# Two attention layers' output stage: turns handed on sooner, x moved in tiles, and every output tile behind the last attention step

## The reference

```python
def _L0_attn_ref(x, w_q, w_k, w_v, w_o):
    ...
    q, k, v = (proj(w_q), proj(w_k), proj(w_v))
    scores = jnp.einsum('bhqd,bhkd->bhqk', q, k) / jnp.sqrt(jnp.float32(D_K))
    attn = jax.nn.softmax(scores, axis=-1)
    out = jnp.einsum('bhqk,bhkd->bhqd', attn, v)
    out = out.transpose(0, 2, 1, 3).reshape(B, S, HIDDEN)
    return jnp.einsum('bse,oe->bso', out, w_o)
...
x = L0_attn_x
x = x + _layernorm(_L0_attn_ref(_layernorm(x, axis=-1), ...), axis=-1)
x = x + _layernorm(_L0_ffn_ref(_layernorm(x, axis=-1), ...), axis=-1)
x = x + _layernorm(_L1_attn_ref(_layernorm(x, axis=-1), ...), axis=-1)
x = x + _layernorm(_L1_ffn_ref(_layernorm(x, axis=-1), ...), axis=-1)
```

## Time and profile before

| | |
|---|---|
| median of 3 runs | 2146.65 us (2146.11 to 2153.83) |
| the profiled execution | 2145.93 us, of which 2144.0 us are the span from its first to its last instruction |
| PE busy | 1921.5 us (90% of the span), 11664 products |
| DVE / ACT / POOL busy | 1422.2 us (66%) / 1142.0 us (53%) / 211.3 us (10%) |
| mean granted clock of PE | 0.958 of full speed |
| DMA | 178.16 MB, mean 83 GB/s |

### The profile page before, as it was taken

One profiled execution on the slowest core, in us unless ns is written; L12 is line 12 of the kernel. 1 busy time (PEld: TensorE's weight loads), 2 busy tenths in 40 slices (PEclk: granted clock), 3 DMA queues, 4 the chain that ended last, 5 costly groups with the idle time before them and its releaser, 6 DMA issues. The chain is left out here.

```text
span 2144.0 us, 31834 instructions
## 1 busy us (share of the span) xinstructions
PE 1921.5 (90%) x11664; PEld 1087.6 (51%) x11664; DVE 1422.2 (66%) x2444; ACT 1142.0 (53%) x2391; POOL 211.3 (10%) x251
## 2 busy tenths in 40 slices
PE   5999999999999999659999999499999999996585
PEld 4864333333333333347888887364444444443463
DVE  5346979999999997354433231567777787763577
ACT  3214777888887887313322221125677777763143
POOL 0000010000000000330010010100100000002313
PEclk9999999999999999879999999699999999998798
DMA  6582443354335431243010100462633444412411
GB/s 202 158 190 74 66 105 69 56 84 76 63 65 82 75 57 39 76 165 100 16 40 1 40 20 0 143 162 68 137 77 79 81 87 90 80 54 76 171 41 59
DMA packets 133434, 178.16 MB, mean 83 GB/s; under 512 B 48244, under 2 KB 59380, under 8 KB 133136
## 3 DMA queue, kind: packets, MB, share of 16 engines
q1 hardware_dynamic: 132896, 175.38, 35.4%
q0 software_dynamic: 384, 0.77, 0.1%
HBM read 111.21 MB, written 64.36 MB: 82 GB/s over the span
## 5 line engine op out<-in xcount | busy, mean ns | idle before, releaser
L927 DVE TENSOR_REDUCE maxesB<-banksB 128x1 f32<-128x1024 f32 x512 | 602.2, 1216 | 92.4 <-PE banksB L993 92.3
L883 ACT ACTIVATE probsB<-banksB 128x512 f32<-128x512 f32 x1024 | 529.6, 602 | 134.8 <-PE banksB L1004 134.7
L924 DVE CUSTOM_DVE_ANT_0 junkG<-banksG,rampG 128x896 bf16<-128x896 f32 (+7 forms) x512 | 368.2, 756 | 104.1 <-PE banksG L993 95.5
L1004 PE MATMUL banksB<-q_stackB,k_stackB 50*128 50x512 f32 x1024 | 405.1, 473 | 7.8 <-DMA q_stackB<-mpartsB 4.8
L883 ACT ACTIVATE probsG<-banksG 128x512 f32<-128x512 f32 (+3 forms) x768 | 326.2, 492 | 119.6 <-PE banksG L1015 68.4
L993 PE MATMUL banksB<-k_stackB,q_stackB 48*128 48x512 f32 x1024 | 345.7, 443 | 3.7
L1004 PEld LDWEIGHTS banksB<-q_stackB,k_stackB 50*128 50x128 f32 x1024 | 167.6, 185 | 270.5 <-ACT probsB L883 228.1
L1004 PE MATMUL banksG<-q_stackG,k_stackG 54*128 54x512 f32 (+3 forms) x768 | 259.6, 413 | 22.0 <-ACT probsG L883 16.5
L1037 PE MATMUL banksB<-probsB,v_onesB 128*32 128x512 f32 x2048 | 276.0, 611 | 0.0
L993 PE MATMUL banksG<-k_stackG,q_stackG 52*128 52x512 f32 (+3 forms) x768 | 248.2, 409 | 11.0 <-DVE maxesG L924 8.2
L993 PEld LDWEIGHTS banksB<-k_stackB,q_stackB 48*128 48x128 f32 x1024 | 155.0, 186 | 85.0 <-DVE maxesB L927 73.8
(11 more groups left out here) (229 smaller groups left out, 2759.5 us busy)
## 6 DMA issues: line engine op xcount, KB each, us to landing
q_stackB<-q_parts SPq DMA_DIRECT2D x96, 128.0 KB, 6.8
k_stackB<-k_parts SPq DMA_DIRECT2D x96, 128.0 KB, 7.2
q_stackG<-q_parts SPq DMA_DIRECT2D x96, 128.0 KB
q_parts<-partsA SPq DMA_DIRECT2D x16, 512.0 KB, 4.2
k_parts<-partsA SPq DMA_DIRECT2D x16, 512.0 KB, 2.8
turns<-o_copyB SPq DMA_DIRECT2D x32, 256.0 KB
q_parts<-partsF SPq DMA_DIRECT2D x16, 512.0 KB, 2.8
turns<-o_copyG SPq DMA_DIRECT2D x32, 256.0 KB, 3.3
```

Source lines behind the costliest of these rows:

```text
L883: act.activation(probs[:, (i % ring) * GH + h, first:HALF], st_ps[:, n % n_st, first:HALF], ACT.Exp).then_inc(st_used, 1)
L924: dve.tensor_tensor_reduce(junk[:, n % JUNK, 0:width], scores, ramp[:, SEQ - width:SEQ], 1.0, LOWEST, ALU.add, ALU.max, out).then_inc(maxe ...
L927: dve.reduce_max(out, scores, AX.X).then_inc(maxed, 1)
L1004: ins = pe.matmul(st_ps[:, n % n_st, first:HALF], kst[at, it % 3, h % kh, kt * P:(kt + 1) * P], qst[at, it % 3, half, h % GS, first:HALF], ...
```

## The change

- Every turn's results are handed on sooner: on SP, behind `max_rows(t)`, now stand `store_turn(t - 2)`, `fetch(t - 3)`, `store_inverse(t - 4)` and `spread_inverse(t - 5)`, and DVE inverts turn t - 3 in the second step of turn t instead of turn t - 5. The two last pairs but one are divided in the second and fourth step of the last turn.
- `TILES_AHEAD` goes from 4 to 0: all 16 output tiles stand behind the last attention step. The last turn is inverted behind the statistics of tile 2 and divided ahead of the root of tile 4. Tiles 8 to 11 wait for 15 of the 16 pairs, tiles 12 to 15 for all.
- x is loaded and stored in tiles of 128 rows (256 KB) in 8 slots: the first 8 are loaded one an iteration in iterations 1 to 8, the other 8 as slots come free. All stores stand behind `spread_inverse(last)`, and each waits until the one ahead of it is complete.
- wo is loaded in four chunks in iterations 1 to 4, and split at turns 10 to 13.

```diff
--- before.py
+++ after.py
@@ -48,7 +48,7 @@
 SIDES = P // SIDE
 GS = GH // SIDES
 LEAD = 3400
-TILES_AHEAD = 4
+TILES_AHEAD = 0
 ROW_FIXED, STEP_FIXED = 140, 370
 LOWEST = -3.0e38
 JUNK = 8
@@ -191,6 +191,13 @@
         for k, ap in self.aps.items():
             sp.dma_start(self.raw[k][:, :, :], ap.rearrange("(c p) e -> p c e", p=P)).then_inc(self.loaded[k], 16)
 
+    def load_chunk(self, sp, c):
+
+        k = self.order[0]
+        if c:
+            sp.wait_ge(self.loaded[k], 16 * c)
+        sp.dma_start(self.raw[k][:, c, :], self.aps[k][P * c:P * (c + 1), :]).then_inc(self.loaded[k], 16)
+
     def split_high(self, act, keys):
         for k in keys:
             act.wait_ge(self.loaded[k], 16)
@@ -207,8 +214,7 @@
     def split_piece(self, pool, i):
 
         k = self.order[0]
-        if i == 0:
-            pool.wait_ge(self.loaded[k], 16)
+        pool.wait_ge(self.loaded[k], 16 * (i + 1))
         pool.tensor_copy(self.high[k][:, i, :], self.raw[k][:, i, :]).then_inc(self.high_out, 1)
         pool.wait_ge(self.high_out, i + 1)
         pool.tensor_tensor(self.low[k][:, i, :], self.raw[k][:, i, :], self.high[k][:, i, :].bitcast(F32),
@@ -732,14 +738,14 @@
 
             def after_rows(t):
 
-                if 0 <= t - 3 < TURNS:
-                    store_turn(t - 3)
-                if 0 <= t - 4 < TURNS:
-                    fetch(t - 4)
-                if 0 <= t - 6 < TURNS:
-                    store_inverse(t - 6)
-                if 0 <= t - 7 < TURNS:
-                    spread_inverse(t - 7)
+                if t >= 2:
+                    store_turn(t - 2)
+                if t >= 3:
+                    fetch(t - 3)
+                if t >= 4:
+                    store_inverse(t - 4)
+                if t >= 5:
+                    spread_inverse(t - 5)
 
             def load_more():
                 sp.wait_ge(proj.w.ready, proj.w.total)
@@ -775,29 +781,36 @@
                     load_stacks(sp, it + 2)
                 if it == 1:
                     proj.stored_block(sp, NB - 1)
-                    out.w.load(sp)
-                    out.load(sp, 0)
-                    sp.wait_ge(out.x_loaded, 16)
-                    out.load(sp, 1)
-            store_turn(last - 2)
-            fetch(last - 3)
+                if 1 <= it <= DC:
+                    out.w.load_chunk(sp, it - 1)
+                if 1 <= it <= out.SLOTS:
+                    out.load(sp, it - 1)
             fetch(last - 2)
-            spread_inverse(last - 6)
-            store_inverse(last - 5)
-            spread_inverse(last - 5)
+            spread_inverse(last - 4)
+            store_inverse(last - 3)
             store_turn(last - 1)
+            spread_inverse(last - 3)
             fetch(last - 1)
-            for t in range(last - 4, last):
-                store_inverse(t)
-                spread_inverse(t)
-            out.sync(sp, range(0, 1))
+            store_inverse(last - 2)
+            spread_inverse(last - 2)
+            store_inverse(last - 1)
+            spread_inverse(last - 1)
+            early = max(tiles_ahead - 1, 0)
+            for t in range(early):
+                out.store(sp, t)
             store_turn(last)
             fetch(last)
+            for t in range(early):
+                out.load(sp, out.SLOTS + t)
             store_inverse(last)
             spread_inverse(last)
+            for t in range(early, NT):
+                out.store(sp, t)
+                if early <= t - 1 < NT - out.SLOTS:
+                    out.load(sp, out.SLOTS + t - 1)
             sp.wait_ge(m_rows, n_rows * TURNS)
             sp.wait_ge(i_spread, 16 * TURNS)
-            out.sync(sp, range(1, NB))
+            sp.wait_ge(out.stored, 16 * NT)
 
         @block.gpsimd
         def _(pool):
@@ -823,8 +836,8 @@
             def after_split(t):
                 if t >= 8 and t // 2 % 2:
                     divide(t - 8)
-                if 3 <= t < 3 + out.w.count("wo"):
-                    out.w.split_piece(pool, t - 3)
+                if 10 <= t < 10 + out.w.count("wo"):
+                    out.w.split_piece(pool, t - 10)
 
             for dst, src in copies:
                 pool.dma_start(dst, src).then_inc(copied, 16)
@@ -851,12 +864,11 @@
                 if tile_at(i, 2) is not None:
                     out.tile_root(pool, tile_at(i, 2))
                     out.tile_add(pool, tile_at(i, 2))
-                if i == first_of[last] + 5:
-                    divide(last - 5)
-                    divide(last - 4)
+                if i in (first_of[last] + 1, first_of[last] + 3):
+                    divide(last - 5 + (i - first_of[last] - 1) // 2)
             divide(last - 1)
             for t in range(tiles_ahead, NT):
-                if t == tiles_ahead + 2:
+                if t == tiles_ahead + 4:
                     divide(last)
                 out.tile_root(pool, t)
                 out.tile_add(pool, t)
@@ -952,13 +964,12 @@
             for i, (it, half, kt, *_) in enumerate(steps):
                 for n in units_at[i]:
                     maximum(n)
-                if i - 1 == first_of[2 * it + half] and 2 * it + half >= 5:
-                    invert(2 * it + half - 5)
+                if i - 1 == first_of[2 * it + half] and 2 * it + half >= 3:
+                    invert(2 * it + half - 3)
                 if not causal and kt == 0 and i:
                     copy_o(2 * it + half - 1)
-                if i - first_of[last] in (2, 4):
-                    invert(last - 4 + (i - first_of[last] - 2))
-                    invert(last - 3 + (i - first_of[last] - 2))
+                if i - first_of[last] in (3, 5):
+                    invert(last - 2 + (i - first_of[last] - 3) // 2)
                 if tile_at(i, -1) is not None:
                     out.tile_low(dve, tile_at(i, -1))
                 if tile_at(i, 2) is not None:
@@ -969,13 +980,13 @@
                 copy_o(TURNS - 1)
             for t in range(tiles_ahead, NT):
                 out.tile_stats(dve, t, s_ps)
-                if t + 2 < NT and (t + 2) % (NT // BATCH):
+                if t + 2 < NT and t + 2 != NT - TB:
                     out.tile_low(dve, t + 2)
                 if t > tiles_ahead:
                     out.tile_norm(dve, t - 1, s_ps)
-                if t + 2 < NT and (t + 2) % (NT // BATCH) == 0:
+                if t + 2 == NT - TB:
                     out.tile_low(dve, t + 2)
-                if t == tiles_ahead + 1:
+                if t == tiles_ahead + 2:
                     invert(last)
             out.tile_norm(dve, NT - 1, s_ps)
 
@@ -1091,12 +1102,14 @@
 
 
 
+    SLOTS = 8
+
     def __init__(self, sb, load_sb, sems, tag, x, x_out, wo_ap, power):
 
         self.x, self.x_out, self.power = x, x_out, power
         self.on = sb(f"on{tag}", [P, DC, TOK], F32)
         self.w = Weights(load_sb, sems, tag, {"wo": wo_ap})
-        self.xt = load_sb(f"xt{tag}", [P, 2, TB, D], F32)
+        self.xt = load_sb(f"xt{tag}", [P, self.SLOTS, D], F32)
         self.onh = sb(f"onhT{tag}", [P, 3, DC, P], F32R)
         self.onl = sb(f"onlT{tag}", [P, 3, DC, P], F32R)
         self.stats = sb(f"ystats{tag}", [P, 2, 6], F32)
@@ -1108,23 +1121,18 @@
         self.summed, self.meaned, self.padded, self.rooted, self.normed, self.added, self.stored = (sems(n) for n in (
             "y_stats", "y_mean", "y_var_eps", "y_rstd", "y_normed", "x_added", "x_stored"))
 
-    def load(self, sp, nb):
-        sp.dma_start(self.xt[:, nb % 2, :, :], self.x[BLK * nb:BLK * (nb + 1), :].rearrange("(t p) d -> p t d", p=P)
-                     ).then_inc(self.x_loaded, 16)
-
-    def sync(self, sp, blocks):
-        for nb in blocks:
-            sp.wait_ge(self.added, TB * (nb + 1))
-            if nb:
-                sp.wait_ge(self.stored, 16 * nb)
-            sp.dma_start(self.x_out[BLK * nb:BLK * (nb + 1), :].rearrange("(t p) d -> p t d", p=P), self.xt[:, nb % 2, :, :]
-                         ).then_inc(self.stored, 16)
-            if nb + 2 < NB:
-                sp.wait_ge(self.stored, 16 * (nb + 1))
-                sp.wait_ge(self.x_loaded, 16 * (nb + 2))
-                self.load(sp, nb + 2)
-            if nb == NB - 1:
-                sp.wait_ge(self.stored, 16 * NB)
+    def load(self, sp, t):
+        if t:
+            sp.wait_ge(self.x_loaded, 16 * t)
+        if t >= self.SLOTS:
+            sp.wait_ge(self.stored, 16 * (t - self.SLOTS + 1))
+        sp.dma_start(self.xt[:, t % self.SLOTS, :], self.x[P * t:P * (t + 1), :]).then_inc(self.x_loaded, 16)
+
+    def store(self, sp, t):
+        sp.wait_ge(self.added, t + 1)
+        if t:
+            sp.wait_ge(self.stored, 16 * t)
+        sp.dma_start(self.x_out[P * t:P * (t + 1), :], self.xt[:, t % self.SLOTS, :]).then_inc(self.stored, 16)
 
     def tile_piece(self, pe, t, c, y_ps):
 
@@ -1141,8 +1149,10 @@
 
     def tile_high(self, act, t, divided, turns):
 
-        if t % (NT // BATCH) == 0:
```

(10 more changed lines are left out.)

## The result

The changed kernel takes 2131.74 us against 2145.41 us for the kernel before, medians of 16 runs each on the same chip: a ratio of 0.9934, with a 95% interval of 0.9913 to 0.9956. That is about 14 us faster, where I forecast 38.6. The direction was right; the time lies 24 us above the forecast and 5 us above the range. The profiled execution took 2131.5 us, 14.4 less than the one of the kernel before.

A forecast was written before the change was run, and what follows sets the result against it. PE, busy 90%, was taken as the bound, with gains only where it stands still or clocks lower. Layer ends (15.5 and 12.0 us) plus loads (11.1) gave 38.6 us off, 2108 us; range 2101 to 2127.

The forecast's parts named there:

- T: Start of the first output tile behind the attention; forecast at 872.7 us in layer 0 and 1945.25 in layer 1.
- The steps without tiles: End of each layer's attention: without woven output tiles, steps take 2.60 us; 8.4 us sooner in layer 0, 9.7 in layer 1.
- my bound of 10.8: Upper bound for layer 1's gain from steps without tiles: four whole tiles at 2.7 us each.
- the steps are no shorter: Rival: without tiles, ACT or the three score banks hold the steps; 18 us back, 2126 us, chance 0.05.
- Some 10 us ahead of the next row maxima, so nothing waits: Added loads of x and wo in iterations 1 to 8, layer 0: about 0.4 us each on SP, delaying nothing.
- The burst's removal: Iteration 1: no longer loading wo and two blocks of x at once gains 7.3 us in layer 0, 3.8 in layer 1.
- the bursts go but the maxima stay late: Rival: row maxima still come late although the loads are spread; 11 us more, 2119 us, chance 0.08.
- The output stage: Sixteen tiles in a row: 3.18 us each, the last three 2.70; last addition ends at T + 57.2.
- The last turn's chain: Output stage: last turn's store, fetch, inverse and spread are hidden; POOL divides at T + 19.2 with 1.8 us to spare.
- The stores: Output stage, SP: 3.2 us a store between loads, 2.5 after; last one 0.7 us late, then 3.5 us.
- the rival at 2150 us: Rival: stores become the new bound at 4.3 us a cycle, the last issued 21.1 us later per layer; chance 0.12.
- DVE's wait for the sums: Rival: DVE waits for sums in every turn, from a landing of 6.1 us on; 2163 us at 8 us, chance 0.05.

The follow-up runs named there:

- run 10: The changed kernel once more, unedited, on another chip: 2129.92 us, 0.9903 of the kernel before.
- runs 2: The changed kernel with two filler products a step added in the last 10 or 11 attention steps: 2117.51 us, 0.9849 of the kernel before.
- run 7: The changed kernel with loads of x and wo moved behind even turns' row maxima, plus two filler products in each quiet step: 2106.96 us, 0.9794.
- Run 3: The changed kernel with loads of x and wo moved behind the row maxima of even turns, an iteration later: 2119.98 us, 0.9861.
- Run 5: The kernel before with only its loads of wo and x taken apart, moved to iterations 2 to 4: 2137.67 us, 0.9929.

## Why the prediction was wrong

By the profiled executions, 38.6 us were forecast and 14.3 us came (spans of 2144.0 and 2129.7). The 24.3 us between them are these.

| step of the prediction | forecast | measured | difference |
|---|---|---|---|
| layer 0, rows of turn 31, by the loads | 7.3 sooner | 0.1 later | 7.4 |
| layer 0, from these rows to T | 26.6 | 35.46 | 8.9 |
| layer 1, from these rows to T | 28.1 | 36.50 | 8.4 |
| T to the next phase, two layers | 2 x 61.4 | 60.36 + 60.63 | -1.8 |
| layer 1, from its first load to the rows of turn 31, by the loads | 3.8 sooner | 2.4 sooner | 1.4 |

**The steps without tiles: wrong, and the largest part (17.3 us).** "The step behind them, with neither row scores nor tile, takes 2.60 us" was read from one single step that stood behind full ones, and I multiplied it by nine. Where the clock holds, the stretch is right to a tenth of a microsecond in layer 0: 26.6 us in run 10, 26.7 in runs 2 and 7. In layer 1 the true worth is 37.8 - 26.7 = 11.1 us, even above my bound of 10.8. But the change leaves PE waiting for ACT in each of these steps (busy 11.2 of 13.2 us in the window ahead of the fall), and in five such stretches of six it was granted the lower level before the end; filled up, in four of four it was not. I had named "the steps are no shorter" as a rival at 18 us, which is the size that came, and gave it 0.05 since I saw only ACT and the score banks as its cause. The profile of before had the sign that I needed, the 0.91 of rows 9: I had read there that PE loses its clock behind a standstill, and didn't ask it of the stretch that I was thinning out.

**"Some 10 us ahead of the next row maxima, so nothing waits": wrong (7.4 us).** I counted the issue on SP, 0.4 us, and looked for a queue there. The queue is in the DMA engines. The burst's removal brought its 7.3 us, and the new place of the loads took as much. Run 3 gives them back by the place alone: from the rows of turn 1 to those of turn 31 it takes 631.8 us where the changed kernel and the one before take 638.9 and 638.7 (207.37 to 846.25, 207.42 to 846.15), 7 us of the 7.3 forecast. Run 5 shows the same on the kernel before, 631.3 us. In my list this is nearest to "the bursts go but the maxima stay late", with 0.08; its reason against, an idle SP, looked at the same wrong queue.

**The output stage: right.** The loop of DVE and POOL, 3.18 and 2.70 us a tile, gave 47.5 us from the first to the last normalization (936.58 - 889.12), and I had 47.5. The last turn's chain is hidden with the forecast reserve: the reciprocal at T + 11.4 (forecast T + 11.5), the division at T + 19.2 (forecast T + 19.2). The stall of rows 1 is gone.

**The stores: right.** While loads stand between them two stores lie 2.3 to 3.4 us apart, and the last seven have no load between and wait for the additions (17.94 us for seven). (By its own cycles, eight of 3.2 us and seven of 2.5, the prediction should have had the last store 0.4 us late, not 0.7; it is issued as the last addition ends.) So the rival at 2150 us is false: its row of 4.30 us had a spread ahead of it, and here too the first store, just behind the spread at 894.78, held the second back to the end of a group of 4.32 us (from 895.36). The Trainium skill's fit (DMA: Bandwidth & Descriptors, Anatomy of one DMA — SWDGE (gpsimd) path) had 2.6 us for such a cycle as an estimate; the page gives it for DMAs issued by POOL, these are issued by SP, and the 2.3 to 3.4 us of this trace agree all the same. The Trainium skill's rule of 1 MiB or more for the most bandwidth (the same page, Rules for kernel authors) would have led wrong here, for the first load of the next phase is issued 3.3 us behind the last addition, where it was 5.56 us with 1 MB.

**DVE's wait for the sums: right that it doesn't come.** DVE waits twice for sums in layer 0, 11.3 us in all, both near the end (until 858.40 and 866.17), where it has nothing else to do. In a middle turn it never waits for them.

With the two wrong steps mended (run 7) the change is worth about 44 us: what I had summed was there to be had, and the change as made didn't keep it. What makes the clock fall in one stretch and hold in another of the same kernel stays open.

## What to carry to other kernels

Work that lies beside the bound may be what keeps PE's clock up. Before it is moved away, ask what stays for PE in the stretch that is left, and put real work or a few fillers in its place. A transfer isn't free because its issue is: look at the share of the DMA engines at that moment, and place large loads behind the small transfer that somebody waits for, not ahead of it. At a stage's end, what counts is what still stands in the issuing queue ahead of the last result.

## What the runs showed of the hardware

- A small wait costs about double. In the changed kernel 2.3 us of waiting for row maxima made a turn 4.7 us longer (granted clock 0.56 from 321 to 328 us), and in run 10 2.6 us made it 6.0 us (0.50 from 410 to 420 us), 1.6 us 4.0 us.
- With PE busy 0.85 and 0.84 of the time, the clock fell in one execution (0.50 over 23.8 us) and held in another (1.00 over 26.6 us). What decides it stays open. Nor does it differ in quiet steps alone: one turn of layer 1 that no edit touched took 16.3 us at 0.79 in nine profiles and 21.0 us at 0.53 in three.
- Two filler products of 512 columns, put into a wait for ACT, lengthened a step by 0.01 us (2.60 to 2.61), and the clock stayed at 1.00 in all four stretches.
- Loads of 256 KB took 11.8 and 12.0 us to land when issued right behind twelve stack loads, and 5.4 and 5.5 us when issued behind the row maxima (run 3). The stack loads of 128 KB themselves took 8.5 and 8.7 us.
